# A state-space layer with its feed-forward on one core: the gate projection moves into the transposed x's bank, the taps go tile by tile, and TensorE's slot is put in another order

## What is computed

```python
x = _rmsnorm(hidden_states, norm_w)
proj = jnp.einsum('bsd,de->bse', x, in_proj_w)
z = proj[..., :D_INNER]
xBC = proj[..., D_INNER:D_INNER + CONV_DIM]
...
xc = jax.lax.conv_general_dilated(xc, conv_w[:, None, :], window_strides=(1,), padding='VALID', dimension_numbers=('NCH', 'OIH', 'NCH'), feature_group_count=CONV_DIM)
xc = xc + conv_b[None, :, None]
xBC = _silu(jnp.swapaxes(xc, 1, 2))
...
dt = jax.nn.softplus(dt_raw + dt_bias)
A = -jnp.exp(A_log)
dA = jnp.exp(dt * A)

def step(h, inp):
    x_t, B_t, C_t, dA_t, dt_t = inp
    h = dA_t[..., None, None] * h + (dt_t[..., None] * x_t)[..., None] * B_t[:, :, None, :]
    y_t = jnp.einsum('bhpn,bhn->bhp', h, C_t)
    return (h, y_t)
...
y = y + D[None, None, :, None] * xs
y = y.reshape(B_, S, D_INNER)
g = y * _silu(z)
gg = g.reshape(B_, S, G, GROUP_SIZE)
var = jnp.mean(jnp.square(gg), axis=-1, keepdims=True)
g = (gg * jax.lax.rsqrt(var + EPS)).reshape(B_, S, D_INNER) * gate_norm_w
out = jnp.einsum('bsd,de->bse', g, out_proj_w)
return residual + out
```

## Time and profile before

| | us |
|---|---|
| runs of the kernel before, median of 3 | 1501.82 (1501.54 to 1502.5) |
| the profiled execution, its own time | 1501.18 |
| span in its profile | 1499.5 |
| first scan of a slot (b = 0, n = 4) starts at | 112.5 |
| last scan (in the drain) starts at | 1337.6 |

### The profile page before, as it was taken

The page is one execution under the profiler, slowest core; times in us unless marked ns, Lnnn a source line. Parts: engine busy times, 40 slices in busy tenths (PEclk is TensorE's granted clock), DMA queues, the critical chain, the costliest instruction groups (busy, mean ns, idle before and its releaser), DMA issues. The chain is left out here.

```text
span 1499.5 us, 43588 instructions
## 1 busy us (share of the span) xinstructions
PE 1160.9 (77%) x15222; PEld 827.5 (55%) x15222; DVE 1088.2 (73%) x2325; ACT 778.5 (52%) x2090; POOL 893.6 (60%) x848
## 2 busy tenths in 40 slices
PE   2347778888788878888888788878888888886887
PEld 2225555555556555655565556555555555563455
DVE  8737677777677767776777667766777777765895
ACT  2545455555455545555555455554555555541444
POOL 2613466767466666665767557665766766796231
PEclk9986699989898998898999889898999999996899
DMA  5331212222212212221222212222222222210201
GB/s 131 140 91 44 57 50 66 58 58 59 79 58 50 61 57 72 58 57 53 72 58 58 66 49 64 52 57 76 58 58 58 72 58 58 58 58 24 99 28 36
DMA packets 88882, 94.41 MB, mean 63 GB/s; under 512 B 22736, under 2 KB 66384, under 8 KB 88400
## 3 DMA queue, kind: packets, MB, share of 16 engines
q1 hardware_dynamic: 84432, 89.37, 21.6%
q10 hardware_dynamic: 4224, 2.10, 0.5%
HBM read 81.99 MB, written 9.44 MB: 61 GB/s over the span
## 5 line engine op out<-in xcount | busy, mean ns | idle before, releaser
L1068 DVE SCALAR_TENSOR_TENSOR conv<-bank,cw,conv 128x511 f32<-128x511 f32 (+2 forms) x576 | 427.4, 744 | 104.0 <-ACT conv L777 103.4
L632 POOL TENSOR_TENSOR gated<-gated,rbs 128x512 f32<-128x512 f32 x128 | 163.7, 1280 | 239.4 <-ACT rbs L831 239.4
L1321 PE MATMUL bank<-xn_hi,w_hi 128*128 (+1 forms) x320 | 173.7, 543 | 138.7 <-DVE conv L1068 138.7
L777 ACT ACTIVATE conv<-bank,cb_bias,cw 128x512 f32<-128x512 f32 x192 | 146.6, 778 | 250.8 <-PE bank L1325 250.2
L1030 DVE SCALAR_TENSOR_TENSOR gated<-chan,dskip,bank 128x256 f32<-128x256 f32 x256 | 111.5, 477 | 176.9 <-ACT bt L823 71.0
L792 ACT ACTIVATE xdt<-bank,dt_all 128x64 f32<-128x64 f32 x1024 | 223.2, 333 | 14.5 <-DVE xw L1057 13.3
L617 POOL TENSOR_TENSOR gated<-gated,gate 128x512 f32<-128x512 f32 x128 | 164.0, 1281 | 100.2 <-DVE gated L1030 100.0
L1082 DVE SCALAR_TENSOR_TENSOR hpk<-hpk,pend,bank 128x64 f32<-128x64 f32 x768 | 210.1, 274 | 5.5
L610 POOL TENSOR_TENSOR lm<-lm,cbs 128x512 f32<-128x512 f32 x128 | 163.8, 1280 | 50.8 <-ACT cbs L816 38.5
L1367 PE MATMUL bank<-ident_t,chan 128*128 128x128 f32 x512 | 122.9, 325 | 89.2 <-issue 26.2
L1346 PE MATMUL bank<-xw,bt 64*64 64x64 f32 x3584 | 173.2, 238 | 0.0
(11 more groups left out here) (175 smaller groups left out, 1704.6 us busy)
## 6 DMA issues: line engine op xcount, KB each, us to landing
spread<-decay_scratch SPq DMA_DIRECT2D x256, 128.0 KB, 3.3
spread<-product_scratch SPq DMA_DIRECT2D x256, 128.0 KB, 3.8
lm<-in_L_attn_in_proj_w SPq DMA_DIRECT2D x1, 2048.0 KB, 8.9
xn_scratch<-chan SPq DMA_DIRECT2D x4, 512.0 KB, 5.1
r_stage<-residual_scratch SPq DMA_DIRECT2D x8, 256.0 KB, 3.1
x_scratch<-r_stage SPq DMA_DIRECT2D x8, 256.0 KB, 3.6
cbs<-x_scratch SPq DMA_DIRECT2D x8, 256.0 KB, 2.8
gated<-x_scratch SPq DMA_DIRECT2D x1, 2048.0 KB, 7.9
```

What stands on the lines that cost most here:

```text
L632: gp.tensor_tensor(gated[:, v % 2, m % R, :], gated[:, v % 2, m % R, :], rbs[:, :], ALU.mult).then_inc(normed, 1)
L1068: V.scalar_tensor_tensor(out=conv[:, ci % 4, shift:S], in0=tile_bank(b, n, t)[:, 0:S - shift], scalar=cw[:, q, t, KW - 1 - shift:KW - shif ...
L1321: MM(out_b, wh, hi, start=True, stop=False)
```

## The change

Instructions are the same in number and size but for one: `vtok` is written by DVE and no longer by ACT. What changes is banks, order and waits.

- z goes into bank 5, where the transposed x stood, at the end of the slot, after `xdt` is done; the next slot's transposes wait for the gate's silu (`gate_done`). Banks 0 and 1 then hold convolution tiles alone.
- Taps go tile by tile, and `ORDER` fixes how state steps (digits) and taps (T) alternate on DVE; the weighing comes ahead of them.
- A slot projects only the second of its own tiles; the first one of the next slot is projected at the slot's end (`project_next`).
- The small job stands directly behind the states. Its copy on ACT no longer waits for `y_ready`; TensorE waits for it in `y_inputs`, ahead of y intra (or of the last pass of the second tile). In slots 7 and 15 it waits there for two more DVE operations.
- The variance products go into columns 448 to 455 of the state bank, between the two halves of the states; DVE reads them.
- ACT's order: first tap start, silu, small copies, `ocm` (slot 14), second tap start, `xdt`, `rexp`, square, gate.

```diff
-            for shift in range(1, KW):
-                for t in PLAN[r]:
+            for t in PLAN[r]:
+                for shift in range(1, KW):
...
+ORDER = {0: "0123456", 1: "01T23T456T", 2: "0T1T2T3T4T56T"}
...
-            return proj_bank[PROJ.index((n, t)) % 2]
+            return proj_bank[CONV_ORDER.index((n // R, t)) % 2]
...
+        var_at = NS * (NBLK - 1)
...
-                if back(b, n, LAG_Y) is not None:
-                    bb, m = back(b, n, LAG_Y)
-                    after(act, y_ready, SLOTS, bb, m)
                 if r == 0 and ssd is not None:
...
+                if n == XO_SLOT - 1 and back(b, n, SLOTS) is not None:
+                    bb, _ = back(b, n, SLOTS)
+                    after(act, out_step, SLOTS, bb, SLOTS - 1)
+                    after(act, xo_ready, 1, bb, -1)
+                    act.activation(ocm[:, :], out_bank[:, :], ACT.Copy).then_inc(out_copied, 1)
+                if real and len(PLAN[r]) == 2:
+                    start_tile(PLAN[r][1])
...
-                    act.activation(gate[:, m % R, :], tile_bank(b, n, "z")[:, :], ACT.Silu).then_inc(gate_done, 1)
+                    act.activation(gate[:, m % R, :], xt_bank[:, :], ACT.Silu).then_inc(gate_done, 1)
...
+                    after(dve, var_ready, UNITS, bb, v)
+                    if state is not None:
+                        after(dve, s_ready, SLOTS, *state)
+                    after(dve, rstd_done, UNITS, bb, v - 1)
+                    V.tensor_scalar(vtok[:, :], s_bank[:, var_at:var_at + 2 * CH], 1.0 / (DI // G), EPS, ALU.mult, ALU.add).then_inc(var_copied, 1)
+                taps = [(shift, t) for t in PLAN[r] for shift in range(1, KW)] if real else []
+                for turn in ORDER[len(taps) // (KW - 1)]:
+                    if turn == "T":
+                        one_tap(*taps.pop(0))
+                    elif state is not None:
+                        state_step(int(turn))
...
+            def three_passes(dst, tile, b, done, last_waits=None):
+
+                wh, wl = w_hi[:, tile[0], tile[1], :], w_lo[:, tile[0], tile[1], :]
+                hi, lo = xn_of(xn_hi, b), xn_of(xn_lo, b)
+                MM(dst, wh, hi, start=True, stop=False)
+                MM(dst, wh, lo, start=False, stop=False)
+                if last_waits is not None:
+                    last_waits()
+                MM(dst, wl, hi, start=False, stop=True).then_inc(done, 1)
...
+                    after(pe, tap, NTAP, pb, TAP[pq, pt, KW - 1])
...
+                def y_inputs():
...
                     after(pe, m_done, SLOTS, bb, m)
                     state_there(pe, bb, m)
                     after(pe, cdec_done, SLOTS, bb, m)
+                    if r == 0 and ssd is not None:
+                        cb, cm = ssd
+                        after(pe, cb_copied, 2 * UNITS, cb, 2 * (cm // R) + 1)
...
+                    if n == XN_SLOT and following(b) is not None:
+                        after(pe, lo_done, 2, b, 3)
+                    if n == XO_SLOT and back(b, n, SLOTS) is not None:
+                        after(pe, x1_done, 2, back(b, n, SLOTS)[0], 1)
...
+                def project_next():
+
+                    nb, nn = (b, n + 1) if n + 1 < SLOTS else (following(b), 0)
+                    if nb is None or not real or own_first(nb, nn):
+                        return
+                    project(nb, nn, PLAN[nn % R][0], intra_finished if len(PLAN[r]) == 1 else None)
...
+                    after(pe, silu_done, NCONV, bb, CONV_ORDER.index((mq, 2 + mr)))
+                    after(pe, gate_done, SLOTS, bb, m - 1)
+                    x_transposes(0)
...
+                if real and len(PLAN[r]) == 2:
+
+                    project(b, n, PLAN[r][1], y_inputs)
+                    if yy is not None:
+                        y_intra()
+                    if yy is not None:
+                        intra_finished()
+                    if ssd is not None or st is None:
+                        out_projection()
+                    if yy is not None:
+                        y_inter()
+                else:
+                    y_inputs()
+                    if ssd is not None or st is None:
+                        out_projection()
+                    if yy is not None:
+                        y_intra()
+                    if real:
+                        project_next()
...
+                if ssd is not None:
+                    bb, m = ssd
+                    xdt_there(pe, bb, m)
+                    three_passes(xt_bank[:, :], (m // R, CONVS + m % R), bb, z_ready)
+                if real and len(PLAN[r]) == 2:
+                    project_next()
```

More of the change, by code:

```diff
@@ L1089, in slot @@
                     scan()
[L1090 removed]
                 if ssd is not None:
[L1092 to L1099 removed]
+                    weigh()
                 if n == XN_SLOT and following(b) is not None:
@@ L1108, in slot @@
                     after(dve, xo_ready, 1, bb, 0)
-                    if back(b, n, LAG_Y) is not None:
-                        after(dve, y_ready, SLOTS, *back(b, n, LAG_Y))
                     dve.wait_ge(res_loaded, bb * 16 + 16)
@@ L1320, in project @@
-                hi, lo = xn_of(xn_hi, bb), xn_of(xn_lo, bb)
-                MM(out_b, wh, hi, start=True, stop=False)
-                MM(out_b, wh, lo, start=False, stop=False)
-                if t == "z" and back(b, n, LAG_Y) is not None:
-                    after(pe, y_intra_done, SLOTS, *back(b, n, LAG_Y))
-                MM(out_b, wl, hi, start=False, stop=True).then_inc(z_ready if t == "z" else proj_ready, 1)
+                    pb, pc = (b, ci - 2) if ci >= 2 else (b - 1, ci - 2 + NCONV)
@@ L1386, in slot @@
-                if st is not None:
-                    states(0)
-                if ssd is not None:
-                    x_transposes(1)
-                else:
-                    if st is not None:
-                        after(pe, s_low_done, SLOTS, *st)
-                    out_projection()
-                if st is not None:
-                    states(1)
-                if real:
-                    for t in PLAN[r]:
-                        project(b, n, t, (b, n))
-                if n > LAG_Y or not (isinstance(b, int) and b == 0):
-                    skip_there(pe, *(back(b, n, LAG_Y + 1) or (NB - 1, SLOTS - 1)))
@@ new lines, in variance @@
+                def variance():
+                    bb, m = back(b, n, LAG_VAR)
+                    v = m // R
+                    after(pe, ssum_step, 3 * UNITS, bb, 3 * v + 2)
+                    for c in range(CH):
+                        last = MM(s_bank[:, var_at + 2 * c:var_at + 2 * c + 2], ssum[:, v % 2, P * c:P * c + P], blockones[:, :], start=True, stop=True)
+                    last.then_inc(var_ready, 1)
+                def y_inputs():
+                    if yy is None:
+                        return
@@ L1438, in slot @@
-                if n == XN_SLOT and following(b) is not None:
-                    pe.wait_ge(staged, b * 16 + 16)
-                    for c in range(CH):
-                        last = TR(spare(c // 2)[:, P * (c % 2):P * (c % 2) + P], xn_stage[:, c, :], ident)
-                    last.then_inc(xnt_ready, 1)
-                if n == XO_SLOT and back(b, n, SLOTS) is not None:
-                    bb, _ = back(b, n, SLOTS)
-                    after(pe, out_copied, 1, bb, 0)
-                    for c in range(CH):
-                        last = TR(xo_half(b, c // 2)[:, P * (c % 2):P * (c % 2) + P], ocm[:, P * c:P * c + P], ident)
-                    last.then_inc(xo_ready, 1)
@@ L1475, in slot, with intra_finished @@
                     last.then_inc(y_ready, 1)
-                if r == 0 and back(b, n, LAG_VAR) is not None:
-                    bb, m = back(b, n, LAG_VAR)
-                    v = m // R
-                    after(pe, ssum_step, 3 * UNITS, bb, 3 * v + 2)
-                    if ssd is not None:
-                        xdt_there(pe, *ssd)
-                    for c in range(CH):
-                        last = MM(xt_bank[:, 2 * c:2 * c + 2], ssum[:, v % 2, P * c:P * c + P], blockones[:, :], start=True, stop=True)
-                    last.then_inc(var_ready, 1)
+                def intra_finished():
+                    if yy is not None:
+                        after(pe, y_intra_done, SLOTS, *yy)
```

267 lines of the change are left out of this document (128 added, 139 removed).

## The result

The changed kernel takes 1454.99 us (median of 4, 1454.03 to 1456.37) where the kernel before takes 1502.16: ratio 0.967 [0.964, 0.971], 47 us faster. The forecast was 1384 with a range from 1325; 70 us of its 117 did not come. Measured again beside later runs (e9) the ratio is 0.962 [0.958, 0.967].

A forecast was written before the change was run, and what follows sets the result against it. Latency between engines, with TensorE and DVE taking turns in two-tile slots, bounds the kernel. 31 units fall from 1197 to 984 us, plus 46 extras and 50 clock: 1080, saving 117, so 1384 us; range 1355 to 1412, 8 in 10 1325 to 1435.

The forecast's parts named there:

- The tap waits and the `rbs` wait: TensorE's 138.7 us of waits for DVE taps and POOL's 239.4 us for ACT's small copy were to go.
- The two new waits at r = 0: TensorE waits 0.86 for ACT's B-C copy, then 0.7 for the gate's silu before the next transposes; period 9.4 us.
- three signs named for a failure: Transposes waiting for the gate in every slot; DVE never idling; PEclk in the loop 1.00 or under 0.85.
- The unit: Four slots at full clock, 9.4 + 2 x 7.75 + 6.85 = 31.75 us, against 38.6 before.
- only the third pass of the second tile waits for it, ending at 3.45: Slots r = 1 and 2: the small copy returns at about 3.25 and holds up just this pass; period 7.75 us.
- The extras: Added waits per sequence in slots 7 (2.3 us), 15 (2.1) and 14 (2.2): 6.6, seven times, 46 us.
- the clock: TensorE at half clock 4.4 us a unit, losing 1.6 a unit, 50 us over 31 units; bounds 0 and 3.0.
- The ends: Prologue, drain and feed-forward, outside the 31 full units: left at zero change.
- The rule on the clock: Skill's rule that idle gaps lower TensorE's clock; read as full clock with gaps of 1 us or less, giving 1334.
- rival of 1334: The clock holds: less idling keeps TensorE at 2.4 GHz, 984 + 46, so 1334 us; chance 0.20, with anything faster.
- z wants the bank of the slot's first tile: In two-tile slots z waits for that tile's last tap, fifth of six; TensorE idles 2.44 us in the slot shown.
- The slower rival: Bank 5's loop runs through ACT's queue; a gate late by d costs 124 d, 1545 us at d = 1.3; chance 0.06.

The follow-up runs named there:

- e9: The changed kernel measured again beside later runs, nothing altered: 1449.7 us, ratio 0.962 to the kernel before.
- e7: Changed kernel with every third tap of a tile on DVE cut to its first 64 columns: 1452.0 us, ratio 0.965.
- e13: Changed kernel with the second of ACT's two small copies cut to 16 columns at r = 0, 1, 2, except in the first sequence: 1420.9 us, ratio 0.942.
- e2: Changed kernel with every engine's loop over the middle sequences written out: 1424.3 us, ratio 0.944 to the kernel before.
- e6: Kernel before with the loops over sequences written out on all five engines: 1474.4 us, ratio 0.982.
- e14: Kernel before with taps tile by tile alone (e10), plus its loops over sequences written out: 1317.4 us, ratio 0.874.
- e3: Changed kernel with z ahead of y inter in the one-tile slots (r = 0 and 3): 1381.2 us, ratio 0.915 to the kernel before.
- e4: As e3, with the out projection and two passes of the next tile also ahead of the wait for the small copy: 1325.7 us, ratio 0.878.
- e8: Changed kernel with e4's order, the loops written out and the `ocm` copy at the end of ACT's slot 14: 1256.8 us, ratio 0.838.
- e10: Kernel before with the tap order alone changed, tile by tile, z's bank and all else as before: 1361.9 us, ratio 0.904.

## Why the forecast was wrong, step by step

*Right.* The tap waits and the `rbs` wait go. The two new waits at r = 0 (0.78 and 0.69 where 0.86 and 0.7 were worked out), and with them the period of 9.4 at full clock (744.16 to 753.54 in the trace: 9.38). The gate is covered at r = 1 and 2 and exposed at r = 3 and 0. DVE is not the pace, as e7 shows. `xdt` is ready ahead of z except in slot 14. None of the three signs named for a failure showed: the transposes waited for the gate 60 times and not in every slot, DVE idled before the weighing (115.0 us), and PEclk in the loop was 0.92. The signs did not cover what went wrong.

*The unit: 33.1 at full clock, not 31.75; 42 us.* Slots r = 1 and 2 were counted at 7.75 and take 8.31 (0.56 each), r = 3 at 6.85 and takes 7.13. The step that failed is "only the third pass of the second tile waits for it, ending at 3.45": the copy does come back at 3.3, but then a whole pass follows, and y intra starts at 3.84. That is 0.39 of the 0.56; the rest is 0.08 from y intra to the out projection and 0.11 in that (1.06, where I had 0.95), less 0.02 in what follows. e13 shows the place: with the copy ending 0.2 earlier, both slots are 0.2 shorter.

*The boundary: about 31 us, left out.* A period averaged over 127 slots of before held it; a unit written out by hand did not. e2, e6 and e14 gain 31, 27 and 45 us without the jumps, of which slots 15 and 0 hold 22, 26 and 29; in e2 and e14 the rest comes in slots where no jump stands.

*The extras and the clock: 96 forecast, 94 measured, by luck.* The 124 slots last 1151.6, less 31 x 33.1 = 1026 for the units and 31 for the boundary: 94. The sum fits, but its parts do not. Against their full-clock lengths the slots n = 7, 14, 15 and 0 take 103 us more; without the 31 of the boundary that is 72, where the extras were put at 46, because the clock also falls in and behind them. The other slots r = 0 lose 17 and the first four 5, 22 in all, where the clock was put at 50. The lower clock was granted for 207 us, 6.7 a unit, where the forecast had 4.4.

*The ends: 5 us*, forecast at zero: 4 from the last full slot to the end (187.5 against 183.5) and 1 before the first. And before's 31 units last 1203 by the transposes, not 1197, which is 6 us in the other direction. In sum 42 + 31 - 2 + 5 - 6 = 70.

*The rule on the clock.* In the changed kernel PEclk is 0.92 from 200 to 1200 us. The 23 averaged slots r = 0 have no wait of 1 us or more, yet 12 of them have some of the lower clock and take 10.8 to 12.1, while the other 11 take 9.5 at most. The Trainium skill, "TensorE: Matmul & The Clock Gate", section "HAM oscillation — how this bites in real kernels", blames idle gaps alone. The forecast read it so that gaps of 1 us or less leave the clock full, and by that these 12 slots should not be; the trace disagrees. (Its rival of 1334 would have missed by the unit and the boundary in any case.) With one of the two waits covered (e3) the clock fell in 3 of the 23, with both (e4, e8) in 1, so short waits matter too, here among small products.

*What the forecast didn't ask.* It put the tap order and the bank of z together as one step ("z wants the bank of the slot's first tile") and priced the package. The rows showed that the fifth tap was the cause; to make it the third took these waits from 138.7 to 40.9 us (e10), and the other route, another bank for z, brings two waits that the order of the taps does not. The slower rival (the loop through bank 5) was looked for in ACT's queue; it is real, but as 0.69 in half of the slots, as the forecast itself had it, and at r = 0 to cover it gained 1.6 a slot (e3), 0.96 of that at full clock.

Open: why the clock falls in about half of the slots r = 0 of the changed kernel and not in the others, which have the same waits, and nearly never once both waits are covered; also why a covered idle time of 0.69 gives 0.96 at full clock. e10's slots r = 1 are alike: those at full clock take about 9.1 and those with some of the lower clock 9.6 or more, and what picks them was not tried. Nor was the bank of z tried without the new order of TensorE's queue.

## What to carry to other kernels

When several edits aim at one wait, price each alone: the cheapest may take nearly all of it, and each of the others can bring its own waits. A sum by slots must be made in the same way for both kernels, with the loop's jump and the slots with extras as lines of their own. Where TensorE waits for a copy, put work with no need of it in between; here the cover was worth more than the wait where the clock fell (1.6 us a slot for an idle time of 0.69).

## What was not expected of the hardware

- **The jump back of a loop with a long body** (a whole sequence of 16 slots) shows as 3 to 4 us of idle time on TensorE, DVE and ACT at once (3.79, 3.99, 2.97 above, all "issue"). To write the loop out and so remove the five jumps gains 31 us in the changed kernel, 27 in the one before and 45 in e10.
- **TensorE's clock** fell to its lower level, 1.2 GHz, with waits of only 0.7 to 1.0 us between small products. In another slot r = 0 of the changed kernel, with the same wait of 0.78 as at 748.35 above, the out projection takes 1.85 us instead of 1.12; in e2, in the slot that begins with the wait of 0.78 shown there, it takes 2.04:

```profile
781.47 1.85 PE L1339 MATMUL bank<-gated,w_out 128*128 128x512 f32 x2 [0.78 <-ACT cbs L794]
```

```profile
802.99 2.04 PE L1339 MATMUL bank<-gated,w_out 128*128 128x512 f32 x2 [0.98 <-ACT cbs L794]
```

  The granted clock is 0.92 in the changed kernel from 200 to 1200 us and 1.00 in e8 from 200 to 1000, with the same products.
- **A named releaser can be the wrong one of several**: 0.37 us under the name of DVE's state step became 0.17 when ACT's copy was shortened by 0.2 (e13).
